# Zero rows up to a contraction of 128 in the node stage and the feed-forward products of a four-layer graph network

## The reference, cut to what matters

```python
# layers 0..2, for a node that no edge enters; a is the node's attribute
out_s = (xs @ Wsc0) * a / sqrt(64)
out_v = einsum('nuc,uw->nwc', xv, Wsc1) * a / sqrt(32)
x = layernorm(x + concat(out_s, out_v))
# layer 3, for a node that no edge enters
x = node_input + merge(proj_bs, 0)
s2, v2 = eq_ln(x, ln2_w0, ln2_b0, ln2_w1)
fs, fv = s2 @ f1_ws + f1_bs, einsum(v2, f1_wv)      # 64 -> 192, 32 -> 64 vectors
sc = silu(fs[:, :128]); fv = fv * sigmoid(fs[:, 128:])
x = layernorm(node_input + x + merge(sc @ f2_ws + f2_bs, einsum(fv, f2_wv)))
```

## Time and profile before

| what | value |
|---|---|
| median of 3 runs | 12,945.26 us (12,937.16 to 12,947.41) |
| profiled execution, own time | 12,941.25 us |
| its span | 12,939.5 us |
| mean granted TensorE clock | 0.704 of full |
| PE busy | 11,360.1 us (88%) |
| weight loads busy | 10,419.3 us (81%) |
| DVE busy | 8,158.8 us (63%) |
| ACT busy | 4,423.0 us (34%) |
| POOL busy | 5,973.5 us (46%) |
| node stage, about | 31 to 5,490 us of the span |

### The profile page before, as it was taken

One profiled execution on the slowest core, in us unless ns is written; L12 is line 12 of the kernel. 1 busy time (PEld: TensorE's weight loads), 2 busy tenths in 40 slices (PEclk: granted clock), 3 DMA queues, 4 the chain that ended last, 5 costly groups with the idle time before them and its releaser, 6 DMA issues. The chain is left out here.

```text
span 12939.5 us, 239328 instructions
## 1 busy us (share of the span) xinstructions
PE 11360.1 (88%) x58771; PEld 10419.3 (81%) x58771; DVE 8158.8 (63%) x40524; ACT 4423.0 (34%) x16207; POOL 5973.5 (46%) x8005
## 2 busy tenths in 40 slices
PE   8999999999999999978878888788876888885998
PEld 7999999999999999967767777677765777775888
DVE  4555555555555555567766666566666888886776
ACT  3444444444444444422222222122222222221222
POOL 2333333333333333366766666566664444442443
PEclk5555555555555555589987878777777888887999
DMA  2222222222222222222221111111111111111111
GB/s 62 72 73 73 73 73 73 73 73 73 73 73 73 73 72 73 66 52 55 55 47 44 43 43 43 40 43 42 43 40 35 40 39 39 40 40 39 54 53 48
DMA packets 919771, 722.88 MB, mean 56 GB/s; under 512 B 453930, under 2 KB 871438, under 8 KB 919328
## 3 DMA queue, kind: packets, MB, share of 16 engines
q1 hardware_dynamic: 721696, 522.17, 14.7%
q0 software_dynamic: 197632, 196.80, 6.4%
HBM read 363.73 MB, written 360.00 MB: 56 GB/s over the span
## 5 line engine op out<-in xcount | busy, mean ns | idle before, releaser
L668 DVE SCALAR_TENSOR_TENSOR nodes_z<-bank,nodes_z 125x162 f32<-125x162 f32 x2400 | 816.0, 382 | 1473.6 <-PE bank L807 1473.5
L127 PE MATMUL bank<-ident 128*128 128x128 f32 x10000 | 1598.0, 314 | 93.8 <-PEq L876 59.0
L127 PEld LDWEIGHTS bank<-ident 128*128 128x128 f32 x10000 | 1546.9, 230 | 158.5 <-issue 59.6
L807 PE MATMUL bank<-self_v,nodes_v_t 97*125 97x98 f32 x4800 | 1634.6, 444 | 0.0
L805 PEld LDWEIGHTS bank<-self_s,nodes_s_t 65*125 65x125 f32 x4800 | 1351.2, 332 | 69.7 <-issue 1.1
L805 PE MATMUL bank<-self_s,nodes_s_t 65*125 65x65 f32 x4800 | 1337.2, 381 | 0.9 <-ACT nodes_v_t L733 0.9
L807 PEld LDWEIGHTS bank<-self_v,nodes_v_t 97*125 97x125 f32 x4800 | 1303.0, 331 | 0.0
L743 ACT ACTIVATE nodes_x<-nodes_z 125x161 f32<-125x161 f32 x2400 | 1006.8, 426 | 818.6 <-DVE nodes_z L668 818.6
L1140 POOL DMA_INDIRECT edge_rows<-table,edge_ends_now x832 | 1029.5, 1237 | 395.2 <-POOL edge_ends_now L1133 203.1
L626 POOL TENSOR_SCALAR nodes_x<-nodes_z,nodes_factor,nodes_offset 125x161 f32<-125x161 f32 x800 | 374.7, 478 | 1289.1 <-DVE nodes_offset L687 1289.1
L1183 POOL DMA_INDIRECT table<-edge_new,edge_into_now x600 | 740.3, 1234 | 482.5 <-issue 441.4
(11 more groups left out here) (486 smaller groups left out, 33424.9 us busy)
## 6 DMA issues: line engine op xcount, KB each, us to landing
table<-nodes_z SPq DMA_DIRECT2D x1200, 160.2 KB
nodes_z<-rows SPq DMA_DIRECT2D x400, 160.2 KB
out<-nodes_res SPq DMA_DIRECT2D x400, 156.2 KB
nodes_v_t<-x_t SPq DMA_DIRECT2D x400, 94.7 KB
edge_dst_row<-dst SPq DMA_DIRECT2D x300, 122.1 KB
dest_rows<-kept SPq DMA_DIRECT2D x100, 316.4 KB
nodes_s_t<-x_t SPq DMA_DIRECT2D x400, 63.5 KB
kept<-att_keep SPq DMA_DIRECT2D x100, 218.8 KB
```

The source lines that it names most:

```text
L127: pe.matmul(banks[2 * ((n + lead) % LANES) + odd][:, 0:128], w["ident"][:, :], w["ident"][:, :], start=True, stop=True)
L668: ins = v.scalar_tensor_tensor(z[:, l + 1, k, 0:A + 1], banks[2 + n % 2][0:P, o:o + A + 1], z[:, l, k, A:A + 1], z[:, l, k, 0:A + 1], ALU. ...
L807: ins = pe.matmul(banks[2 + n % 2][0:P, o + MEAN:o + A + 1], xv[:, n, c], w[f"self_v{l}"][:, :], start=False, stop=True, skip_group_check= ...
```

## The change

Tiles and weights that feed these products are made 128 partitions high, the added partitions are set to zero once, and the products then read all 128. Copies, loads and the smaller products that share a weight name their own rows. Products of the node stage that had 65, 96 or 97 rows of contraction, and those of the feed-forward part in both stages that use it, have 128 afterwards. The transposes (125 rows) stay. The sets to zero stand at the head of the two stages, and SP, ACT and PE wait for them there (`ready` has to be 2, not 1).

```diff
@@ ffn_buffers
-            ("s_t", [S + 1, lanes, W]),
-            ("v_t", [V, lanes, W]),
+            ("s_t", [128, lanes, W]),
+            ("v_t", [128, lanes, W]),
...
-            ("hid_v2", [S + 1, lanes, W]),
+            ("hid_v2", [128, lanes, W]),
@@ ffn_copy_turned
-    act.activation(f["s_t"][:, n, :], a[0:S + 1, 0:W], ACT.Copy)
-    act.activation(f["v_t"][:, n, :], a[0:V, W:2 * W], ACT.Copy).then_inc(t["act"][n], 1)
+    act.activation(f["s_t"][0:S + 1, n, :], a[0:S + 1, 0:W], ACT.Copy)
+    act.activation(f["v_t"][0:V, n, :], a[0:V, W:2 * W], ACT.Copy).then_inc(t["act"][n], 1)
@@ prepare_weights
-                        ("f1_s", [S + 1, 256]), ("f1_v", [V, 256]), ("f2_v01", [128, V]), ("f2_v2", [S + 1, F]),
+                        ("f1_s", [128, 256]), ("f1_v", [128, 256]), ("f2_v01", [128, V]), ("f2_v2", [128, F]),
...
-                            ("self_s", [S + 1, S + 1]), ("self_v", [V + 1, V + 2]), ("lin_s", [S + 1, 2 * S]),
+                            ("self_s", [128, S + 1]), ("self_v", [128, V + 2]), ("lin_s", [S + 1, 2 * S]),
...
+            v.memset(w["f1_s"][:, :], 0.0)
@@ all_nodes
-    s0_t = sb("nodes_s0_t", [S + 1, lanes, W])
-    v0_t = sb("nodes_v0_t", [V + 1, lanes, W])
-    s_t = sb("nodes_s_t", [S + 1, lanes, W])
-    v_t = sb("nodes_v_t", [V + 1, lanes, W])
+    s0_t = sb("nodes_s0_t", [128, lanes, W])
+    v0_t = sb("nodes_v0_t", [128, lanes, W])
+    s_t = sb("nodes_s_t", [128, lanes, W])
+    v_t = sb("nodes_v_t", [128, lanes, W])
...
-            sp.wait_ge(ready, 1)
+            sp.wait_ge(ready, 2)
...
-            v.memset(ffn["hid_v2"][S:S + 1, :, :], 1.0)
-            v.memset(z[:, 1:4, :, ROW - 1:ROW], 0.0).then_inc(ready, 1)
+            v.memset(z[:, 1:4, :, ROW - 1:ROW], 0.0)
+            for x in (s0_t, v0_t, s_t, v_t, ffn["s_t"], ffn["v_t"]):
+                v.memset(x[:, :, :], 0.0)
+            v.memset(ffn["hid_v2"][:, :, :], 0.0).then_inc(ready, 1)
+            v.wait_ge(ready, 1)
+            v.memset(ffn["hid_v2"][S:S + 1, :, :], 1.0).then_inc(ready, 1)
...
+            act.wait_ge(ready, 2)
...
+            pe.wait_ge(ready, 2)
@@ edges_layer (the weights are higher now, the product is not)
-                    pe.matmul(bank[0:P, 192:192 + VS], e["ds_t"][:, n, c], w[f"self_s{l}"][:, :],
+                    pe.matmul(bank[0:P, 192:192 + VS], e["ds_t"][:, n, c], w[f"self_s{l}"][0:S + 1, :],
...
@@ attention_nodes
-            v.memset(ffn["hid_v2"][S:S + 1, :, :], 1.0)
+            for x in (ffn["s_t"], ffn["v_t"], ffn["hid_v2"]):
+                v.memset(x[:, :, :], 0.0)
             v.memset(e["sums"][:, :, :, :], 0.0).then_inc(ready, 1)
+            v.wait_ge(ready, 1)
+            v.memset(ffn["hid_v2"][S:S + 1, :, :], 1.0).then_inc(ready, 1)
...
+            act.wait_ge(ready, 2)
...
-            pe.wait_ge(ready, 1)
+            pe.wait_ge(ready, 2)
```

More of the change, by code:

```diff
@@ L452, in _ @@
             for c in range(3):
-                v.tensor_scalar(w["f1_v"][:, c * 64:(c + 1) * 64], f1v[:, :], w["mod3"][:, c:c + 1], w1[:, 0:1],
+                v.tensor_scalar(w["f1_v"][0:V, c * 64:(c + 1) * 64], f1v[:, :], w["mod3"][:, c:c + 1], w1[:, 0:1],
                                 ALU.mult, ALU.mult)
@@ L477, in _ @@
             for l in range(3):
-                v.tensor_copy(w[f"self_v{l}"][:, 0:V + 1], banks[l][0:V + 1, 0:V + 1])
+                v.tensor_copy(w[f"self_v{l}"][0:V + 1, 0:V + 1], banks[l][0:V + 1, 0:V + 1])
                 v.tensor_copy(w[f"self_s{l}"][S:S + 1, :], banks[l][S:S + 1, 128:128 + S + 1])
@@ L576, in load_x @@
                 rows = bass.ds(i * T + J * n, J)
-                sp.dma_start(s0_t[:, n, :].rearrange("f (j p) -> f j p", j=J), x_t[0:VS, rows, :]
+                sp.dma_start(s0_t[0:VS, n, :].rearrange("f (j p) -> f j p", j=J), x_t[0:VS, rows, :]
                              ).then_inc(x_loaded[n], 16)
-                sp.dma_start(v0_t[:, n, :].rearrange("f (j p) -> f j p", j=J), x_t[MEAN:X, rows, :]
+                sp.dma_start(v0_t[0:V + 1, n, :].rearrange("f (j p) -> f j p", j=J), x_t[MEAN:X, rows, :]
                              ).then_inc(x_loaded[n], 16)
@@ L731, in copy_turned @@
                     act.wait_ge(t["pe"][n], count_at(t, i + 1, "pe", f"turned{l}"))
-                    act.activation(s_t[:, n, :], banks[n % 2][0:S + 1, 0:W], ACT.Copy)
-                    act.activation(v_t[:, n, :], banks[n % 2][0:V + 1, W:2 * W], ACT.Copy
+                    act.activation(s_t[0:VS, n, :], banks[n % 2][0:S + 1, 0:W], ACT.Copy)
+                    act.activation(v_t[0:V + 1, n, :], banks[n % 2][0:V + 1, W:2 * W], ACT.Copy
                                    ).then_inc(t["act"][n], 1)
@@ L1486, in add_up @@
                     c, bank = slice(j * P, (j + 1) * P), banks[2 * n + j]
-                    pe.matmul(bank[0:P, 192:192 + VS], e["ds_t"][:, n, c], w[f"self_s{l}"][:, :],
+                    pe.matmul(bank[0:P, 192:192 + VS], e["ds_t"][:, n, c], w[f"self_s{l}"][0:S + 1, :],
                               start=True, stop=True)
                     ins = pe.matmul(bank[0:P, 192 + MEAN:192 + X], e["dv_t"][:, n, c],
-                                    w[f"self_v{l}"][:, 0:X - MEAN], start=False, stop=True, skip_group_check=True)
+                                    w[f"self_v{l}"][0:V + 1, 0:X - MEAN], start=False, stop=True, skip_group_check=True)
                 one(ins, n)
```

## The result

The changed kernel took 12,611.60 us (median of 3 runs, 12,567.56 to 12,621.69) where the one before took 12,945.26: a ratio of 0.9735, 95% interval 0.9699 to 0.9771. That is faster by 2.7%. The forecast was 10,715 us, so 1,897 us of the forecast saving of 2,230 did not come, and the time lies outside the range.

What follows compares the result with a forecast made beforehand. PE alone at half clock was taken to bound the node stage, DVE next. 12,941 - 2,284 (turns) + 15 (sets to zero) + 40 (filling) = 10,712 us, adjusted to the runs' median and stated as 10,715; range 10,470 to 11,210.

Steps and rivals of the forecast that it cites:

- The clock and the rows: Node stage: rows in use, zeros included, not busy share, set PE's clock; padding lifts it from 0.50 to 1.00.
- Rows cost nothing: Node-stage products and weight loads: 128 rows take at most 1 ns more per record, 14 us in 400 turns.
- DMA goes from 24% to some 42%, which leaves room: Node stage: DMA's mean busy share rises with the faster turns but does not bound them.
- Who is next: Step on the node stage's next bound: DVE longest at 7.22 us a turn, PE just behind; 7.2 to 9.0 us.
- 400 x (13.51 - 7.8): Node stage: saving over 400 turns that fall from 13.51 to 7.8 us each, 2,284 us.
- DVE as the next bound, 7.8 us a turn at 93%: Node stage: with PE at full clock, DVE's 7.22 us of work bounds a turn, taken as 7.8 us.
- Sets to zero: Heads of node and destination stages: added memsets cost 12 and 2.6 us, together +15 us.
- Filling, +40: Start of the node stage: first turns gain little while the pipeline fills; 0 to 70 us, taken as 40.
- Later stages: Destination stage and edge layers: no gain; a change over 10 us would mean something shared was overlooked.
- Rival 2: Node stage: clock alternates at a mean of 0.79, turns of 9.48 us, total 11,370 us; chance 0.07.
- Rival 1: Node stage: step order, not DVE's work, bounds a turn at 9.0 us, total 11,207 us; chance 0.13.
- Rivals 3 and 4: Node-stage clock stays low: only memsets remain, 12,960 us, chance 0.05; or padded loads also slow it, 13,003 us, chance 0.03.

Runs made afterwards that it cites:

- f2_before_split: Kernel before, without padding, with the 97-row load cut into 96 + 1 rows: 12,928.75 us, ratio 0.9990.
- e4_rows_back: Changed kernel, high tiles and sets to zero kept, but every product reads only its own 65, 96 or 97 rows: 12,962.47 us, ratio 1.0016.
- g2_mult_rows_back: f3_after_split_early with the products of `multiply` reading only their own 65 and 97 rows, feed-forward ones still padded: 10,933.14 us, ratio 0.8448.
- f3_after_split_early: Changed kernel with the 97-row load cut into 96 + 1 and the loads 5.8 plan units earlier: 10,935.33 us, ratio 0.8448.
- h1_spread: f3_after_split_early plus seven rounds in each loop pass and the five 125-row transfers cut into 120 + 5: 10,581.27 us, ratio 0.8174.
- f1_after_split: Changed kernel with only the 97-row load cut into 96 + 1 rows: 11,452.92 us, ratio 0.8844.
- e1_after_early: Changed kernel with every node-stage step but the load set 5.8 plan units later, so loads are issued earlier: 12,109.72 us, ratio 0.936.

## Why the prediction was wrong

**What bounded the kernel: right.** PE alone at half clock, in turns of 13.51 us. `f2_before_split` confirms it from the other side: loads that are faster move the kernel before by 0.1%.

**The clock and the rows: right.** The rows that a product reads go with the clock and zeros count (`e4_rows_back`). One premise was weaker than it was told: that the identity products "brought the clock up" isn't in the clock column, which reads 1.00 before they begin at 32.02 us. Only their spacing points to a rise, 9 records from 32 to 34 us and 21 from 38 to 40.

```profile
20.00:30.00 10.00, 3.66 (x14) 2.30 (x14) 6.04 (x37) 0.00 (x0) 0.00 (x0) 1.00 0.00 1
```

"Rows cost nothing" holds: the products of 65 and 97 rows in `g2_mult_rows_back` take 261 and 287 ns, those of 128 rows in `f3_after_split_early` 261 and 286, both at a clock of 0.95, forecast at 250 and 290. That PE would have 1.00 throughout did not hold in the changed kernel: PE waited in each turn, and the mean was 0.81.

**"DMA goes from 24% to some 42%, which leaves room": this step failed.** In "Who is next" only engines with a busy row were set against each other, and DMA was judged by its mean share over 16 engines. The share was low, and it stayed at 25% in the changed kernel, yet the loads took 8 us from issue to use and were issued only behind `store1`. The trace of before had this loop (3006.48 to 3020.01 us, above): 5.54 us from sum to load and 7.99 from load to sum. Only the first part can shrink with a faster PE, and it shrank to 4.36, which was not to be read there; but the second part alone, if the loads need it, puts a turn at 8 us or more, above the 7.8 of the forecast. The loop of the changed kernel has 4.36 + 8.24 = 12.60 us. The term "400 x (13.51 - 7.8)" was therefore 400 x (13.51 - 12.58): 372 instead of 2,284 us.

**DVE as the next bound, 7.8 us a turn at 93%: right once the loads are out of the way.** `h1_spread` has 7.60 us with DVE busy 1,855.78 of 2,000 us, which is 93%, and 7.06 us of work in a turn where 7.22 was taken. It has more than the loads out of the way, for its loop has seven rounds in a pass. With the loads alone repaired, `f3_after_split_early` has 8.55 us, inside the forecast's 7.2 to 8.6, and 7.58 between the stops, which the prediction did not have. That the share is the very 93% is partly luck, as that figure was chosen between two ends. "PE below 95%" did not hold: it is at 97%, with 7.41 us busy in a turn where the sum from pairs of starts gave 6.95. So the runs don't say which of the two bounds it.

**Sets to zero: about right.** The forecast was +15; `e4_rows_back`, which has them and the slow clock, is 22 us above the kernel before of its own comparison, 12,940.56 (by its interval 9 to 34 us). DVE's groups in the first 100 us have eight of them, seven more than before, each 1,725 ns; two of the lines:

```profile
L655 DVE MEMSET nodes_s_t<- 128x2000 f32 x2 | 3.5, 1725 | 0.7 <-issue 0.7
...
L658 DVE MEMSET ffn_hid_v<- 1x2000 f32 x1 | 1.7, 1725 | 0.5 <-DVE ffn_hid_v L656 0.5
```

**Filling, +40: not seen.** No run shows the term by itself. In `h1_spread` the turns (-2,364) and the sets to zero (+15) would give 10,591 us without it, and 10,581 were measured.

**Later stages: right.** The node stage ends some 370 us earlier, so the window of the earlier trace rows for edge layer 0 has to move with it, to 5,230 to 6,130 us. It then reads as before but for half a microsecond of PE:

```profile
5230.00:6130.00 900.00, 777.41 (x5257) 663.85 (x5257) 673.27 (x3185) 269.01 (x959) 630.83 (x718) 1.00 0.24 55
```

**The rivals.** Rival 2, the alternating clock, had the sign of it: the mean is 0.81, near its 0.79. But it made the clock the cause. It is the effect: with faster loads alone (`f1_after_split`) the clock is 0.95. Rival 1, a fixed order, was the right kind, as the place of the loads in it costs some 500 us, but its measure, the 1.05 of other stages, missed the mechanism. Neither had the loads in it. Rivals 3 and 4 needed the clock to stay at 0.50.

## What to carry to other kernels

Before an engine that covers everything else is made faster, list the loops that pass through a DMA (the release of its issue, its latency, its first user, and the work from there to the next issue) and set their length beside the engines' busy times; a mean DMA share says nothing against such a loop. Look at the row counts of the transfers: here 97 rows cut into 96 + 1 took 1,159 us off the changed kernel, with the same bytes. And a gain that does not come may be there behind one wait. The change with both edits of the loads is 2,007 us faster than the kernel before, the change alone 334; of the edits of the loads without the change, the split gave 14 us and the earlier loads cost 66.

## What the runs showed of the hardware that was not expected

- Rows of zeros count for the granted clock. With 36 of 56 matmul records of a turn at 65 to 97 rows it was 0.50 for 5,380 us; with 12 of them at 128 instead, and the loads out of the way, 0.95, as with all 36.
- Twelve transposes in a turn did not keep `h1_spread` from 0.99. The Trainium skill ("TensorE: Matmul & The Clock Gate", section "Part 4: PE-mode transpose") says that transposes don't engage the full clock. The mix here has it, and the transposes run faster in it (L797 of `f3_after_split_early` 284 ns, L788 before 415); transposes alone were not run.
- Transfers of the same bytes differ by their row count: 53 + 44 rows cost 478 us more over the kernel than 96 + 1. What held up the loads of `e1_after_early` shows in no mean share (0.27), but in SP's issue time, 5.13 us for one load.
- In `f3_after_split_early` each pass of the loop over the rounds ends in a stop of about 5.2 us, and the clock is 0.50 for some microseconds behind it. With seven rounds in a pass there are 5 such stops in 2,000 us instead of 29.
- What such a stop costs depends on the step that it falls on: the kernel before has it without a wait of PE, and loads issued earlier moved it to a step that PE needs, which made that kernel 0.5% slower (1.0034 to 1.0068).
